# Key and query norms from squares in channel rows summed by products with ones; value estimates copied to memory once

## What is computed

```python
q = short_conv(x @ Wq.T, conv_q).reshape(Bsz, Tlen, NH, DK)     # short_conv ends in silu
k = short_conv(x @ Wk.T, conv_k).reshape(Bsz, Tlen, NH, DK)
v = short_conv(x @ Wv.T, conv_v).reshape(Bsz, Tlen, NH, DV)
v_hat = jnp.einsum('bthk,vk->bthv', k, Wsv)
e = v_hat - v
s_l2 = jnp.sqrt(jnp.sum(e * e, -1) + EPS_STAT)
s_l1 = jnp.sum(jnp.abs(e), -1)
cos_den = jnp.sqrt(jnp.sum(v_hat * v_hat, -1) + EPS_STAT) * jnp.sqrt(jnp.sum(v * v, -1) + EPS_STAT) + EPS_STAT
s_cos = 1.0 - jnp.sum(v_hat * v, -1) / cos_den
# beta and amp come from a small MLP on (s_l2, s_l1, s_cos)
r = k / jnp.maximum(jnp.linalg.norm(k, axis=-1, keepdims=True), 1e-12)
qn = q * jax.lax.rsqrt(jnp.sum(q * q, -1, keepdims=True) + L2_EPS)
kn = k * jax.lax.rsqrt(jnp.sum(k * k, -1, keepdims=True) + L2_EPS)
# then the recurrence over tokens with qn, kn, v, the decay g and beta
```

## Time and profile before

| what | us |
|---|---|
| three timed runs | 1580.26, 1563.80, 1574.29 |
| their median | 1574.29 |
| the profiled execution | 1571.55 |
| its span, first to last instruction | 1569.7 |
| mean granted TensorE clock over the span | 0.94 of full speed |

### The profile page before, as it was taken

The page is one execution under the profiler, slowest core; times in us unless marked ns, Lnnn a source line. Parts: engine busy times, 40 slices in busy tenths (PEclk is TensorE's granted clock), DMA queues, the critical chain, the costliest instruction groups (busy, mean ns, idle before and its releaser), DMA issues.

```text
span 1569.7 us, 28651 instructions
## 1 busy us (share of the span) xinstructions
PE 1360.0 (87%) x9424; PEld 1050.0 (67%) x9424; DVE 1060.1 (68%) x1981; ACT 807.1 (51%) x2597; POOL 687.8 (44%) x991
## 2 busy tenths in 40 slices
PE   7999757778989889898898898898977889899993
PEld 5777524557767767777676676687766667757772
DVE  5744366778868778889788888897774621265445
ACT  1122127576776766867767668678574332011220
POOL 0277700355354452554644535535455430005772
PEclk9899967899999999999999999999988989989997
DMA  9233320011120220211211311111013213242334
GB/s 359 61 104 103 115 99 20 16 43 34 36 61 17 56 71 15 58 30 46 67 32 31 84 30 32 45 48 51 17 46 110 88 46 148 103 209 71 105 102 174
DMA packets 130960, 117.04 MB, mean 75 GB/s; under 512 B 58944, under 2 KB 115328, under 8 KB 130048
## 3 DMA queue, kind: packets, MB, share of 16 engines
q1 hardware_dynamic: 121216, 90.20, 18.2%
q0 software_dynamic: 9024, 24.65, 5.4%
q10 hardware_dynamic: 576, 0.34, 0.1%
HBM read 80.30 MB, written 34.87 MB: 73 GB/s over the span
## 4 chain that ended last, share of the span: by engine, by line
PE 67%; DVE 15%; ACT 6%; issue 5%; DMA 3%; POOL 2%; DVEq 0%; SPq 0%; POOLq 0%; ACTq 0%
PE proj L1241 9%; DVE big L2829 6%; PE chain L556 5%; PE low L1383 5%; PE tree L1383 5%; PE gates L534 4%; PE low L534 3%; PE proj L1281 2%; PE proj L1287 2%; PE chain L1469 2%; PE tree L1427 2%; PE proj L1515 2%; PE tree L1452 2%; PE proj L471 2%; DVE x L903 2%
## 5 line engine op out<-in xcount | busy, mean ns | idle before, releaser
L3549 POOL TENSOR_TENSOR big<-big 128x512 f32<-128x512 f32 (+6 forms) x112 | 60.4, 539 | 378.2 <-PE tree L1392 123.5
L2829 DVE SCALAR_TENSOR_TENSOR big<-proj,pall,big 128x1022 f32<-128x1022 f32 x129 | 164.4, 1274 | 13.9 <-ACT big L2109 7.8
L1241 PE MATMUL proj<-xT,wqkv 128*128 128x512 f32 x344 | 158.8, 605 | 16.3 <-DVE big L2829 15.6
L2985 DVE TENSOR_TENSOR KQ<-KQ,big 128x1024 f32<-128x1024 f32 x112 | 150.3, 1342 | 17.3 <-PE low L1355 8.3
L980 POOL DMA_INDIRECT inv<-xn_scr,gidx x94 | 91.3, 971 | 135.2 <-DVE sidx L841 107.1
L3551 POOL TENSOR_TENSOR big<-big 128x512 f32<-128x512 f32 x112 | 145.4, 1298 | 0.0
L1241 PEld LDWEIGHTS proj<-xT,wqkv 128*128 128x128 f32 x344 | 63.2, 194 | 82.8 <-issue 63.1
L986 POOL DMA_INDIRECT y_scr<-inv,sidx x94 | 92.8, 987 | 37.0 <-issue 22.5
L626 ACT COPY big<-proj 128x256 f32<-128x256 f32 x94 | 35.2, 374 | 125.9 <-PE proj L523 125.8
L3563 POOL TENSOR_TENSOR prodw<-D,W 64x15 f32<-64x15 f32 (+7 forms) x240 | 89.4, 373 | 18.8
L1383 PE MATMUL low<-KQ,big 128*128 128x128 f32 x640 | 91.1, 286 | 7.6 <-POOL big L3551 4.0
(11 more groups left out here) (311 smaller groups left out, 3649.2 us busy)
## 6 DMA issues: line engine op xcount, KB each, us to landing
big<-in_w_ex SPq DMA_DIRECT2D x2, 4864.0 KB, 20.8
big<-in_w_ex SPq DMA_DIRECT2D x2, 4256.0 KB, 18.7
big<-y_scr SPq DMA_DIRECT2D x8, 1024.0 KB, 8.2
m_img<-big SPq DMA_DIRECT2D x16, 512.0 KB, 3.2
inv<-t_img SPq DMA_DIRECT2D x16, 512.0 KB, 4.2
big<-t_img SPq DMA_DIRECT2D x16, 512.0 KB, 5.1
o_scr<-obuf SPq DMA_DIRECT2D x15, 512.0 KB, 4.0
wqkv<-in_wqkv SPq DMA_DIRECT2D x16, 384.0 KB, 3.8
```

Source lines behind the costliest of these rows:

```text
L1241: m = te.matmul(place(h, j)[:, b, :], wqkv[:, h % 2, j, k, :], xT[:, k, b * T:(b + 1) * T], start=(k == 0), stop=(k == KB - 1))
L2829: ve.scalar_tensor_tensor(conv[:, :, d:T], place(h, j)[:, :, 0:T - d], pall[:, h, 4 * j + 3 - d:4 * j + 4 - d], conv[:, :, d:T], ALU.mult, ...
L2985: ve.tensor_tensor(kr, kr, dl, ALU.mult).then_inc(mkq.sem, 1)
```

## The change

Norms of k and q: the squares are now taken in channel rows, one activation of 128x1024 each, and the sums over channels are made on PE by products of the squares (as weights) with a column of ones, widened to 4 equal columns. p_kk and p_qq (8 transposes each) go; one p_norms of 16 products stands where p_qq stood. norms_out copies the 16 wanted columns from PSUM to kq2. Value estimates: v_guess_rows copies v_hat from PSUM to memory once (128x1024), where vhat_sq stood; err, vhat_sq and v_sq work from that copy or overwrite it, so vhat_sq now waits for err and v_sq for vhat_sq. k_sq is issued right after silu_k; q_sq stands where k_sq stood in most turns; vhat_sq moves to just before v_sq; norms_out stands at q_sq's former place.

```diff
-        ones = sb("ones", [P, 1])
+        ones = sb("ones", [P, 4])
+        k_squares, v_guess, q_squares = sq[:, 1, :], sq[:, 2, :], cut(9216, 1024)
@@ PE
-            def p_kk(h):
-                te.wait_ge(*silu.of(h, 1))
-                te.wait_ge(*prod.of(h))
-                to_rows(cvk[:, h % 2, :], kk)
-            def p_qq(h):
-                te.wait_ge(*silu.of(h, 3))
-                te.wait_ge(*ksq.of(h, 1))
-                to_rows(cvq[:, h % 2, :], kk)
+            def p_norms(h):
+                te.wait_ge(*vh2.of(h, 1))
+                te.wait_ge(*ksq.of(h, 2))
+                for i, squares in enumerate((k_squares, q_squares)):
+                    for c in range(BN):
+                        at = 4 * (i * BN + c)
+                        m = te.matmul(FF[:, 0, at:at + 4], squares[:, c * P:(c + 1) * P], ones[:, :], start=True, stop=True)
+                m.then_inc(kk.sem, 1)
@@ PE, turn(t)
                 i_ty(t - 3, 4)
-                p_kk(t - 1)
                 i_tr(t - 3, 0, 4)
                 g_norm(t - 2, 1)
                 i_tr(t - 3, 1, 4)
                 c_oT(t - 4, 0)
                 c_oT(t - 4, 1)
-                p_qq(t - 1)
+                p_norms(t - 1)
                 i_tx(t - 3, 1, 5)
@@ ACT
+            def v_guess_rows(h):
+                se.wait_ge(*vhat.of(h))
+                se.wait_ge(*v2.of(h - 1))
+                se.copy(wide(v_guess), FF[:, :, :]).then_inc(vh2.sem, 1)
             def vhat_sq(h):
-                se.wait_ge(*vhat.of(h))
+                se.wait_ge(*prod.of(h))
                 se.wait_ge(*cos.of(h - 1, 4))
                 for c in range(BN):
-                    m = se.activation(sq[:, 1, c * P:(c + 1) * P], FF[:, c // NC, c % NC * P:(c % NC + 1) * P], ACT.Square,
-                                      accum_out=red[:, 1, c:c + 1])
+                    v = v_guess[:, c * P:(c + 1) * P]
+                    m = se.activation(v, v, ACT.Square, accum_out=red[:, 1, c:c + 1])
...
             def k_sq(h):
+                se.wait_ge(*kk.of(h - 1))
+                se.wait_ge(*silu.of(h, 1))
+                se.activation(k_squares, cvk[:, h % 2, :], ACT.Square).then_inc(ksq.sem, 1)
             def q_sq(h):
+                se.wait_ge(*kk.of(h - 1))
+                se.wait_ge(*silu.of(h, 3))
+                se.wait_ge(*lt.of(h - 1))
+                se.activation(q_squares, cvq[:, h % 2, :], ACT.Square).then_inc(ksq.sem, 1)
+            def norms_out(h):
                 se.wait_ge(*kk.of(h))
                 se.wait_ge(*rts_.of(h - 1))
+                se.copy(kq2[:, :, :], FF[:, 0, 0:8 * BN].rearrange("p (a c j) -> p a c j", a=2, j=4)[:, :, :, 0]).then_inc(ksq.sem, 1)
@@ ACT, turn(t)
                 silu_k(t - 2)
+                k_sq(t - 2)
                 c_us(t - 5, 1, 0)
                 c_us(t - 5, 0, 0)
...
-                vhat_sq(t - 2)
+                v_guess_rows(t - 2)
                 x_ev(t - 4, 4)
...
                 i_trs(t - 4, 0, 4)
-                k_sq(t - 2)
+                q_sq(t - 2)
                 i_trs(t - 4, 1, 4)
+                vhat_sq(t - 2)
                 v_sq(t - 2)
-                q_sq(t - 2)
+                norms_out(t - 2)
@@ ACT, finish(), head 14
                 x_ev(12, 4)
+                vhat_sq(14)
                 v_sq(14)
-                k_sq(14)
+                q_sq(14)
                 decay(13)
@@ DVE
             def err(h):
-                ve.wait_ge(*vh2.of(h))
+                ve.wait_ge(*vh2.of(h, 1))
+                ve.wait_ge(*vtok_.of(h))
...
+                ve.tensor_tensor(sq[:, 0, :], v_guess, vtok[:, h % 3, :], ALU.subtract).then_inc(eb.sem, 1)
+                ve.tensor_tensor(sq[:, 3, :], v_guess, vtok[:, h % 3, :], ALU.mult).then_inc(prod.sem, 1)
```

More of the change, by code:

```diff
@@ L274, in program @@
         pk, pv, pq, tap0, taps, silu, vT, vtok_, vhat, vh2, v2, e2, eb, prod, red_, kk, ksq, rts_, pw = sigs(
-            pk=1, pv=1, pq=1, tap0=3, taps=9, silu=3, vT=1, vtok=1, vhat=1, vh2=1, v2=1, e2=1, eb=1, prod=1, red=2,
-            kk=2, ksq=2, rts=3, pw=3)
+            pk=1, pv=1, pq=1, tap0=3, taps=9, silu=3, vT=1, vtok=1, vhat=1, vh2=2, v2=1, e2=1, eb=1, prod=1, red=2,
+            kk=1, ksq=3, rts=3, pw=3)
         cos, sT, sTs_, hid_, hidS, z_, zs, bx, bi, tok, sp, spe, rl, lt, ss, dec_, kq, mkq, mdec, msuf, cd_, sub = sigs(
@@ L1553, in begin @@
                 p_v(1)
-                p_kk(0)
-                p_qq(0)
+                p_norms(0)
                 p_q(1)
@@ L1570, in begin @@
                 t_diag(0, 0)
-                p_qq(1)
+                p_norms(1)
                 t_lvl(0, 0, 1)
@@ L1605, in begin @@
                 i_tr(0, 1, 4)
-                p_qq(2)
+                p_norms(2)
                 i_tx(0, 0, 5)
@@ L1752, in finish @@
                 i_ty(11, 5)
-                p_qq(13)
+                p_norms(13)
                 t_diag(12, 0)
@@ L1817, in finish @@
                 i_tr(12, 0, 4)
-                p_qq(14)
+                p_norms(14)
                 i_tr(12, 1, 4)
@@ L1893, in finish @@
                 t_diag(14, 1)
-                p_qq(15)
+                p_norms(15)
                 c_oT(12, 0)
@@ L2351, in begin @@
                 silu_k(0)
+                k_sq(0)
                 tap_q(0)
@@ L2356, in begin @@
                 v_rows(0)
+                v_guess_rows(0)
                 vhat_sq(0)
@@ L2359, in begin @@
                 tap_v(1)
-                k_sq(0)
+                q_sq(0)
                 e_sq(0)
-                q_sq(0)
+                norms_out(0)
                 exp_set(0)
@@ L2369, in begin @@
                 silu_k(1)
+                k_sq(1)
                 silu_v(1)
@@ L2378, in begin @@
                 soft_log(0)
+                v_guess_rows(1)
+                decay(0)
                 vhat_sq(1)
-                decay(0)
                 v_sq(1)
-                k_sq(1)
+                q_sq(1)
                 e_sq(1)
-                q_sq(1)
+                norms_out(1)
                 powers(1)
@@ L2463, in finish @@
                 silu_k(12)
+                k_sq(12)
                 exp_set(0)
@@ L2496, in finish @@
                 m_put(10, 0, 6)
-                vhat_sq(12)
+                v_guess_rows(12)
                 x_ev(10, 4)
@@ L2504, in finish @@
                 i_trs(10, 0, 4)
-                k_sq(12)
+                q_sq(12)
                 i_trs(10, 1, 4)
+                vhat_sq(12)
                 v_sq(12)
-                q_sq(12)
+                norms_out(12)
                 e_sq(12)
@@ L2522, in finish @@
                 silu_k(13)
+                k_sq(13)
                 c_us(10, 0, 0)
@@ L2555, in finish @@
                 m_put(11, 0, 6)
-                vhat_sq(13)
+                v_guess_rows(13)
                 c_os(10, 0, 3)
@@ L2565, in finish @@
                 i_trs(11, 1, 4)
-                k_sq(13)
+                q_sq(13)
                 x_ev(11, 5)
                 o_pow(10)
+                vhat_sq(13)
                 v_sq(13)
-                q_sq(13)
+                norms_out(13)
                 i_trs(11, 0, 5)
@@ L2587, in finish @@
                 silu_k(14)
+                k_sq(14)
                 c_us(11, 0, 0)
@@ L2620, in finish @@
                 o_sq(11)
-                vhat_sq(14)
+                v_guess_rows(14)
                 m_put(12, 0, 6)
@@ L2631, in finish @@
                 k_rows(12, 1)
-                q_sq(14)
+                norms_out(14)
                 e_sq(14)
@@ L2657, in finish @@
                 silu_k(15)
+                k_sq(15)
                 c_os(12, 0, 1)
@@ L2683, in finish @@
                 o_sq(12)
-                vhat_sq(15)
+                v_guess_rows(15)
                 x_ev(13, 4)
@@ L2687, in finish @@
                 decay(14)
+                vhat_sq(15)
                 v_sq(15)
@@ L2693, in finish @@
                 i_trs(13, 1, 4)
-                k_sq(15)
+                q_sq(15)
                 e_sq(15)
-                q_sq(15)
+                norms_out(15)
                 powers(15)
```

31 lines of the change are left out of this document (5 added, 26 removed).

## The result

The changed kernel takes 1651.5 us (median of four, 1644.0 to 1657.3) where the kernel before takes 1572.4 on the same chip: 1.051 times as long, 95% interval 1.047 to 1.054. The forecast was slower, 1621, with a range to 1640: the direction is right, and the loss of 79 us is half as large again as the 50 forecast. The profiled execution after is 1644.0, the fastest of its four (span 1641.6); that of before has a span of 1569.7. The two traces thus differ by 72; the other 7 lie between executions and no trace shows them.

A forecast was written before the change was run, and what follows sets the result against it. PE, busy 87% of the span, was taken as the bound, ACT (51%) not. Profiled 1571.55 + 20 for the queue + 30 for the clock = 1621.5, taken as 1621; own range 1602 to 1640, 8-in-10 range 1585 to 1640.

The forecast's parts named there:

- Steady queue: PE in steady turns: p_norms 3.24 for p_qq's 1.00, starting 1.73 earlier; +0.5 a head, 3.5, and 4.0 for heads 9 to 11.
- err, the copies, k_sq behind silu_k: DVE and ACT: err about 1.1 earlier, ACT net about -0.6 a head, c_us pushed by 1.0 but hidden before c_ko.
- One fall behind nearly each p_norms: Behind most p_norms the clock drops to 0.50 for 3.3 or 6.6, turn's mean 0.92 to 0.97.
- the clock holds: Rival: p_norms too short to make the clock fall, only the queue's 20 is lost, 1592; chance 0.22.
- The replaced transposes didn't count: Rival: p_norms' products count as PE load, four steady clock falls vanish, 11 back from 1592, so 1581; chance 0.04.
- the term for the clock: Behind p_norms of heads 2 to 14: 2.3 lost for each of 13 heads, 30 in all, bounds 0 and 43.
- begin(): Head 0: p_norms behind q_sq ends at 259.5, 4 later, of which 3 reach tap_q and stats_rows; head 1: +0.5.
- finish(): Heads 13 to 15: +2.3, +3.8 (decay's start about 2.1 late, p_norms behind q_sq) and +3 (i_trs slips 1.5, p_norms longer).

The follow-up runs named there:

- mended: Changed kernel with ACT's order in begin() and finish() edited: q_sq(0) right behind v_rows(0), decay(13), q_sq(14) and q_sq(15) ahead of their heads' vhat_sq and v_sq; ratio 1.047.
- wide_fill_warm: Changed kernel with 64 columns of ones, 8 unused transposes where p_kk stood, and unused dense products around p_vT; 1612.3 us, 1.027 of the kernel before.
- half: Changed kernel with 8 products of 8 columns in p_norms instead of 16 of 4, sums over q's squares left out; 1.012 of the kernel before.
- wide64: Changed kernel with ones 64 columns wide instead of 4 in p_norms, norms_out picking every 64th column; 1621.7 us, 1.031 of the kernel before.

## Why the prediction was right or wrong

- **Steady queue**: right in kind. The series takes 3.56 where 3.24 was taken from g_z; a turn without a fall is 0.8 longer, forecast 0.5. For heads 3 to 13 the forecast's terms are 3.5 + 4.0 + 2.3 = 10; the experiments leave 12 to 20, so the term was somewhat low.
- **err, the copies, k_sq behind silu_k**: right. v_guess_rows 1.01, k_sq 1.06, q_sq 1.06, vhat_sq 8 x 0.29; the wait of the transposes for k_sq is gone; c_ko's waits for c_us are 1.0 between 350 and 1010 in both kernels. err starts 1.5 behind p_vhat's end at 1013.93 (1.1 forecast), and i_ts behind it is what i_tr still waits for.
- **One fall behind nearly each p_norms**: right, ten of the eleven steady turns, 3.4 or 6.8 long, 55 us of half clock together where 11 x 4.6 = 51 was meant. The rival "the clock holds" is refuted. The Trainium skill ("TensorE: Matmul & The Clock Gate", HAM oscillation) warns of long idle gaps between matmuls; as the only cause the trace refutes it, since 624.3 to 627 had no gap at all and the turn none longer than 1.65; in the eleven turns only two gaps are longer, 3.2 and 3.7. The turns' mean clock is 0.88 to 1.00 where 0.92 to 0.97 was forecast. "The replaced transposes didn't count" is refuted too: no steady turn got faster. (In the earlier trace rows the clock had been at 1.00 for 34 us, not 5.6, when it fell at 1418.6; 5.6 is how long the 47-column products had run.)
- **The failed step is the term for the clock: "I take 2.3 for each of the 13 heads", one fall per head.** It priced the new falls and took the old ones as fixed. In the eleven steady turns the time at half clock is 96 us after and 20 before, 75 more where the forecast had 51 more. The 24 beyond what was forecast are mostly falls in other places: at p_vT and p_vhat, where the kernel before also has them (four of eleven turns before, 20 us; seven after, 31 us), and in the place of p_kk, now idle (three, 10 us). Each us at half clock cost 0.37 to 0.48, a little under the half that the forecast took, so the price was fair and the count was wrong: 28 to 36 in place of 25. That the old falls multiply is measured; why one turn has a fall at p_vT and the next has none stays open.
- **begin()**: the order was read rightly (p_norms behind q_sq, 255.6), the price wrongly. "It ends at 259.5" took the series at full clock, but the clock fell in the wait of 7 in front of it: 6.8 from start to start instead of 3.24, and p_q(1) 7.2 later, not 4. At g_sT(2) 9.5 was lost; the queue and one fall came to 5.8.
- **finish()**: heads 14 and 15 lost 14.7 where 3.8 + 3 + 2.3 = 9.1 stood. decayed(13) waited 2.3 for decay as forecast (2.1), yet mended shows that this bought nothing. The stretch lost nearly the same in wide_fill_warm (+12.5), so the width of the ones is not it; half has +8.5, so length counts. p_norms(14) at half clock takes 6.96, as the series of head 0. But wide_fill_warm's 17 us less at half clock there gave back only 2.2. What else there is in these 14.7 was not told apart.
- **The rest**: 7 of the 30 missed are the distance of the profiled execution to the median. The forecast's own range was added up wrongly by 2 to 3: from its terms it is 1604 to 1643, which the median exceeds as well.

Sum for the trace: forecast 10 + 25 + 5.8 + 9.1 = 50; measured 47.9 for queue and clock of the steady turns together (12 to 20 and 28 to 36), 9.5 and 14.7, which is 72.

## What to carry to other kernels

An operand that is narrow saves nothing where the weight load sets the pace, and may cost a fall of the clock: widen it, or make the series short. When a change adds light work to PE or leaves a hole in it, recount all the light places of the loop and not only the new one, since the old ones had more falls here too (seven turns in place of four); and price a series behind a long wait at half clock. A gain ahead of a stretch in which PE has little to do may be gone at that stretch's end.

## What the runs showed of the hardware

- 16 fp32 products with 128x128 weights take 3.56 with 4 columns and 3.61 with 64; 8 take 1.78 with 8 columns. The width is all but free here. With 4 columns the clock fell in or behind the series in ten of eleven turns, with 64 columns in none.
- The clock fell to 1.2 GHz while PE was gaplessly busy: 2.7 into the 4-column series that began at 624.34 at full clock.
- A us at half clock cost this kernel 0.37 to 0.48 us (19.5 for 41 in wide64, 34.4 for 92 in wide_fill_warm).
- The same idle stretch at p_vT lets the clock fall in one turn and not in the next (four of eleven turns before, seven after). Filled with unused 128-column products in the kernel before it held there in all eleven, and the four turns that had had a fall became 1.0 to 1.7 shorter.
- Two narrow series of 8 with transposes between them did as much harm (0.93 over the steady middle) as one of 16 (0.93), while one series of 8 alone left 0.97.
